# A decoder layer in one launch: next keys loaded in two halves behind the reciprocals, a later total, direct last sums, reordered fills and a double-buffered output projection

## The reference, cut to what matters

```python
# 1. self attention of the normalised x, blockwise softmax, no mask
attn = softmax(q @ k.T / sqrt(32)) @ v        # q, k, v = layernorm(x) @ w_qkv.T
x1 = x + attn @ w_out.T
# 2. causal cross attention of layernorm(x1) to 154 context rows
x2 = x1 + softmax(mask(q2 @ k2.T / sqrt(32))) @ v2 @ Wo.T + bo
# 3. shared feed forward on all rows, and the best of 8 experts on 1024 selected rows
out = x2 + ffn(layernorm(x2))
```

## Time and profile before

| | us or share |
|---|---|
| median of 3 runs (lowest, highest) | 3226.08 (3216.08, 3235.38) |
| profiled execution: its own time, its span | 3223.79, 3221.8 |
| PE busy | 2954.7, 92% |
| DVE busy | 2101.2, 65% |
| POOL busy | 1751.7, 54% |
| ACT busy | 1608.9, 50% |
| mean granted PE clock, as a share of 2.4 GHz | 0.946 |

### The profile page before, as it was taken

One profiled execution on the slowest core, in us unless ns is written; L12 is line 12 of the kernel. 1 busy time (PEld: TensorE's weight loads), 2 busy tenths in 40 slices (PEclk: granted clock), 3 DMA queues, 4 the chain that ended last, 5 costly groups with the idle time before them and its releaser, 6 DMA issues. The chain is left out here.

```text
span 3221.8 us, 42178 instructions
## 1 busy us (share of the span) xinstructions
PE 2954.7 (92%) x15214; PEld 1739.5 (54%) x15214; DVE 2101.2 (65%) x3804; ACT 1608.9 (50%) x2996; POOL 1751.7 (54%) x750
## 2 busy tenths in 40 slices
PE   8999699999999999999999999959959997999398
PEld 5878355455455454554554555338845554777333
DVE  4332777777777677777777777526638895776323
ACT  2222166666666676666666676722217673222111
POOL 0000179788889798888888888830001101432265
PEclk9999599999999999999999999979969998999589
DMA  7444744745655557457456564438665452342621
GB/s 229 173 179 157 184 103 98 161 99 111 149 112 121 129 106 157 96 107 151 97 114 143 112 143 93 96 105 247 210 169 154 139 146 93 140 169 97 217 68 36
DMA packets 186936, 435.77 MB, mean 135 GB/s; under 512 B 30557, under 2 KB 51966, under 8 KB 166716
## 3 DMA queue, kind: packets, MB, share of 16 engines
q1 hardware_dynamic: 161718, 286.39, 30.7%
q0 software_dynamic: 24448, 145.80, 21.5%
q10 hardware_dynamic: 576, 1.05, 0.1%
HBM read 180.67 MB, written 127.18 MB: 96 GB/s over the span
## 5 line engine op out<-in xcount | busy, mean ns | idle before, releaser
L791 DVE TENSOR_REDUCE part_max<-ps_s 128x1 f32<-128x512 f32 x2048 | 1270.2, 683 | 349.6 <-PE ps_s L692 349.6
L891 ACT ACTIVATE probs<-ps_st 128x512 f32<-128x512 f32 x2048 | 1059.6, 602 | 538.2 <-PE ps_st L711 529.4
L641 POOL TENSOR_TENSOR added<-added,probs 128x2048 f32<-128x2048 f32 x256 | 1181.1, 4614 | 104.6 <-ACT probs L891 82.3
L711 PE MATMUL ps_st<-q_stack,k_stack 98*128 98x512 f32 x2048 | 871.5, 429 | 8.3 <-ACT probs L891 7.0
L692 PE MATMUL ps_s<-k_stack,q_stack 96*128 96x512 f32 x2048 | 831.5, 412 | 24.2 <-POOL max_parts L631 20.7
L711 PEld LDWEIGHTS ps_st<-q_stack,k_stack 98*128 98x128 f32 x2048 | 390.2, 191 | 524.9 <-ACT probs L891 362.0
L722 PE MATMUL ps_pv<-probs,v_sb 128*32 128x512 f32 x4096 | 550.1, 609 | 0.0
L692 PEld LDWEIGHTS ps_s<-k_stack,q_stack 96*128 96x128 f32 x2048 | 399.4, 195 | 121.7 <-DVE part_max L791 36.6
L649 POOL DMA_DIRECT2D probs<-probs x128 | 110.9, 871 | 191.9 <-PE ps_pv L722 167.0
L722 PEld LDWEIGHTS ps_pv<-probs,v_sb 128*32 128x32 f32 x4096 | 80.9, 108 | 163.6 <-ACT probs L891 134.6
L641 POOL TENSOR_TENSOR added<-probs 128x2048 f32<-128x2048 f32 x32 | 146.6, 4581 | 23.9 <-ACT probs L891 23.9
(11 more groups left out here) (273 smaller groups left out, 3534.7 us busy)
## 6 DMA issues: line engine op xcount, KB each, us to landing
probs<-probs POOLq DMA_DIRECT2D x128, 1024.0 KB, 7.2
xq_stack<-q_parts SPq DMA_DIRECT2D x64, 384.0 KB, 4.8
q_parts<-k_stack SPq DMA_DIRECT2D x88, 256.0 KB, 4.0
q_stack<-q_hi SPq DMA_DIRECT2D x64, 256.0 KB, 6.8
k_stack<-k_hi SPq DMA_DIRECT2D x64, 256.0 KB, 9.7
x_in<-in_x_rows SPq DMA_DIRECT2D x8, 1024.0 KB, 7.1
q_hi<-qk_h_out SPq DMA_DIRECT2D x8, 1024.0 KB
q_lo<-qk_l_out SPq DMA_DIRECT2D x8, 1024.0 KB, 6.3
```

Source lines behind the costliest of these rows:

```text
L641: pool.tensor_tensor(added[:, w % 2], left, probs[:, k % RING], ALU.add).then_inc(added_up, 1)
L711: pe.matmul(ps_st[:, n % BANKS], k_stack[0:TOP, w // BPB, j, k * P:(k + 1) * P], q_stack[:, w % 4, j], start=True, stop=True).then_inc(ite ...
L791: dve.tensor_reduce(part_max[:, s:s + 1], ps_s[:, (w * SLOTS + s) % BANKS], AX.X, ALU.max)\
L891: act.activation(probs[:, k % RING, j], ps_st[:, n % BANKS], ACT.Exp, scale=SCALE).then_inc(item_used, 1)
```

## The change

In self attention, the next quad's keys are loaded two heads at a time in the first two units of the current quad and its values in the third, each behind the reciprocals of the unit before and ahead of its store (`load_ahead`); the queries' loads stay at the end of a unit. `INVERT_AT` goes from 9 to 7, `PRODUCT_AFTER` from 5 to 4, chain 0's total from step 8 to 9. In the last unit POOL stops adding after tile 10 and PE sums tiles 11 to 15 directly; chain 1's total comes last. At the stage's start, POOL fills `max_parts` first and the long rows of `k_stack` last, PE starts its scores without waiting for fills, and the identity is converted with a reduce in place of a copy.

In `attention_to_queries`, `a_h` and `a_l` get two buffers, PE projects blocks 0 and 1 before the first transposes, and queries are stored as high and low only (8 transfers for a block, not 12); `cross_attention` reads the high part twice. Three fills of `cross_attention` move from DVE to POOL, and PE waits for them only where it needs them. In `shared_feed_forward`, `bo` is loaded first under its own semaphore, POOL's `add_bias(0, 0)` comes before its fills, and DVE's split of the biases comes after the first norm.

```diff
-    TOTALS_AT = {8: 0, 14: 1}
-    INVERT_AT = 9
-    PRODUCT_AFTER = 5
+    TOTALS_AT = {9: 0, 14: 1}
+    LAST_ADDED = 10
+    INVERT_AT = 7
+    PRODUCT_AFTER = 4
+    LAST_ADDS = ADDED.index(LAST_ADDED)
...
+                def load_ahead(i, w, last):
+                    c, n = w // BPB, w % BPB
+                    if last and c == 1:
...
+                    elif c == 1 or i > 0:
+                        behind = (i, BPB - 1) if c else (i - 1, UPB - 1)
+                        if n < 2:
+                            load_k(2 * i + 1 + c, 1 - c, range(2 * n, 2 * n + 2))
+                        elif n == 2:
+                            sp.wait_ge(pv_done, at(*behind, KT, KT))
+                            load_v(2 * i + 1 + c, 1 - c)
+
+                def body(i, last):
+                    for w in range(UPB):
+                        if not begins(i, w):
+                            reciprocals(*unit_before(i, w))
+                        load_ahead(i, w, last)
+                        if not begins(i, w):
+                            store(*unit_before(i, w))
+                        if not last or w < BPB:
+                            sp.wait_ge(item_done, items(i, w, item(i, w, KT - 1, HEADS - 1) + 1))
+                            load_q(i * UPB + (w + 4), w % 4, w % BPB)
...
-                        for n in range(4, ADDS):
+                        for n in range(4, LAST_ADDS if ends(i, w) else ADDS):
...
-                    if k in TOTALS_AT:
+                    if ends(i, w) and k > LAST_ADDED:
+                        for j in range(HEADS):
+                            mm = pe.matmul(ps_d[j * HD:(j + 1) * HD], ones[:], probs[:, k % RING, j], start=False, stop=False)
+                    elif k in TOTALS_AT:
...
+                def last_totals(i, w):
+                    pe.wait_ge(added_up, at(i, w, ADDS, LAST_ADDS))
+                    for j in range(HEADS):
+                        pe.matmul(ps_d[j * HD:(j + 1) * HD], ones[:], added[:, w % 2, j], start=False, stop=False)
+                    pe.wait_ge(chain_summed[1], at(i, w, 32, 32))
...
-                dve.wait_ge(ident_loaded, 16)
-                dve.tensor_copy(ident_r[:], ident[:]).then_inc(ident_ready, 1)
-                dve.wait_ge(ones_set, 3)
                 for s in range(SLOTS):
                     slot_max(0, 0, s)
                     if s == HALF - 1:
+                        dve.wait_ge(ident_loaded, 16)
+                        dve.tensor_reduce(ident_r[:], ident[:].unsqueeze(2), AX.X, ALU.max).then_inc(ident_ready, 1)
+                        dve.wait_ge(ones_set, 1)
```

The same for the later stages, cut further:

```diff
-        a_h = sb("a_h", [P, DC, BLK], F32R)
+        a_h = sb("a_h", [P, 2, DC, BLK], F32R)
...
-        Q_DMAS = 3 * (P // HD)
+        Q_DMAS = 2 * (P // HD)
...
                 split(0, 0)
                 residual(0, 0)
+                split(0, 1)
                 dve.wait_ge(small_loaded, 32)
                 norm(0, 0)
-                split(0, 1)
+                residual(0, 1)
                 transposed(0, 0, range(TPB))
...
                 project(0, 0)
+                project(0, 1)
...
-                dve.memset(q_stack[ROWS:TOP + 1].bitcast(F32), 1.0).then_inc(rows_set, 1)
-                dve.memset(kt_stack[ROWS:TOP].bitcast(F32), 1.0).then_inc(rows_set, 1)
-                dve.memset(ones[:], 1.0).then_inc(rows_set, 1)
...
-                dve.wait_ge(w_loaded, 6 * 16)
-                dve.wait_ge(consts, 3)
-                dve.tensor_copy(bias_rows[0:1], bias_raw[:]).then_inc(bias_high, 1)
```

More of the change, by code:

```diff
@@ L553, in load_q, with load_k @@
                                      q_units[part][b, g, n]).then_inc(q_loaded[buf], 16)
-                def load_k(quad, buf):
+                def load_k(quad, buf, heads=range(HEADS)):
                     b, g = quad // QUADS, quad % QUADS
-                    for j in range(HEADS):
+                    for j in heads:
                         for row, part in ((0, 0), (1, 0), (2, 1)):
@@ L587, in store @@
                     sp.dma_start(out_units[b, g, w % BPB], attn_out[:, w % 2]).then_inc(out_stored[w % 2], 16)
[L589 to L595, removed]
-                            load_k(i * 2 + (c + 2), c)
-                            sp.wait_ge(pv_done, at(i, w, KT, KT))
-                            load_v(i * 2 + (c + 2), c)
-                        if last and w == BPB - 1:
+                def load_ahead(i, w, last):
+                    c, n = w // BPB, w % BPB
+                    if last and c == 1:
+                        if n == 0:
                             sp.wait_ge(next_w_copied, 32)
@@ L620, in _ @@
                 body(TURNS - 1, True)
+                store(TURNS - 1, UPB - 1)
                 for s in range(2):
@@ L673, in body @@
                                 product(*unit_before(i, w))
+                        if ends(i, w):
+                            product(*unit_before(i, w))
                 body(0)
@@ L737, in added_totals @@
                         mm = pe.matmul(ps_d[j * HD:(j + 1) * HD], ones[:], added[:, w % 2, j], start=False, stop=True)
+                    mm.then_inc(dens_done, 1)
+                def last_totals(i, w):
+                    pe.wait_ge(added_up, at(i, w, ADDS, LAST_ADDS))
+                    for j in range(HEADS):
+                        pe.matmul(ps_d[j * HD:(j + 1) * HD], ones[:], added[:, w % 2, j], start=False, stop=False)
+                    pe.wait_ge(chain_summed[1], at(i, w, 32, 32))
+                    for j in range(HEADS):
+                        mm = pe.matmul(ps_d[j * HD:(j + 1) * HD], ones[:], probs[:, CHAINS[1][-1] % RING, j],
+                                       start=False, stop=True)
                     mm.then_inc(dens_done, 1)
@@ L1069, in _ @@
                 pool.wait_ge(group_low, NBLK * DC)
-                store_part(pool, NBLK // 2 - 1, 1, 1, last_stored)
+                store_part(pool, NBLK // 2 - 1, 1, 1, range(2, 4), last_stored)
             @block.vector
@@ L1126, in body @@
                     if not last:
-                        residual(i2, u2)
+                        if not first(i, u):
+                            residual(i2, u2)
                         norm(i2, u2)
@@ L1149, in split @@
                         act.wait_ge(a_loaded[u], i * 16 + 16 * u)
-                        act.wait_ge(proj_done, count(i, u, TPB, 0))
-                    act.activation(a_h[:], first_a if first(i, u) else a_raw[:, u], ACT.Copy).then_inc(a_high, 1)
+                    if not (isinstance(i, int) and i == 0):
+                        act.wait_ge(proj_done, count(i, u, TPB, -TPB))
+                    act.activation(a_h[:, u], first_a if first(i, u) else a_raw[:, u], ACT.Copy).then_inc(a_high, 1)
                 def transposed(i, u, tiles):
@@ L1216, in body @@
                     i2, u2 = (i, 1) if u == 0 else (i + 1, 0)
-                    if not last:
+                    if not (last or first(i, u)):
                         project(i2, u2)
```

128 lines of the change are left out of this document (69 added, 59 removed).

## The result

The changed kernel takes 3191.67 us (median of 4 runs, 3189.63 to 3194.97) against 3230.73 for the kernel before (4 runs): ratio 0.988, 95% interval 0.9859 to 0.9902. It is 39 us faster; 70.6 were forecast, and 3191.67 lies above the range (3143 to 3184).

The account below looks back on a forecast made before the run. PE was taken to set the pace in self attention, losing 44.6 us at quad starts. That, 16 for the last unit and smaller terms, less collisions and other losses, summed to 70.6 us gained: 3156 us, range 3143 to 3184.

Parts of the forecast that it names:

- The keys in two halves: Self attention: smaller key loads behind the reciprocals remove PE's stalls in the first unit of each new quad; gain 44.6 us.
- The later total: Self attention: chain 0's total one step later removes PE's small waits for links; gain 2 us.
- The opening of self attention: PE waits for its first head's keys instead of POOL's fills; gain 2.5 us (0 to 4).
- The stores behind the projection with the opening of cross attention: Fewer query stores left at the output projection's end, 5 us, and cross attention's first scores waiting for loads alone, 4 us.
- what the half loads collide with: Self attention: key loads briefly overlap chain 1's links; loss 3 us, bounds nothing and 18 us.
- rival A: The collision moves into 18 ordinary units, 1.5 us each: 3179 us; chance 0.10, or 0.04 beyond the point where it turns slower.
- The last unit: End of self attention: shorter link wait, PE's direct sums and no wait for POOL's last adds; gain 16 us (6 to 21).
- Output projection: Its head: projecting block 1 ahead of block 0's transposes leaves these exposed; loss 2 us (1 to 4).
- Feed forward: Its opening: the third projected tile's wait for a residual goes; gain 1.5 us (-1 to 2.5).
- B: Rival: DVE waits at its earlier inversion and PE behind it, 1 us in each of 31 units: 3187 us; chance 0.05.
- C: Rival: quad stalls go, but the last unit gives only 6 us and openings meet the next wait: 3176 us; chance 0.09.
- D: Rival: the 44.6 us at the quad's start have another cause than these loads: about 3200 us; chance 0.04.

Follow-up runs that it names:

- e9: The kernel before with SP's schedule alone changed: keys two heads at a time and values, loaded at the head of the unit; 3187.99 us, ratio 0.987.
- e2: The changed kernel with the loads of keys, values and next weights issued ahead of the unit's reciprocals, not behind them; 3153.30 us, ratio 0.9778.
- e8: e2 with the planner's three numbers set back: chain 0's total at step 8, inversion at 9, product after add 5; 3165.16 us.
- e1: The changed kernel with all loads ahead issued behind the unit's reciprocals and its store, not between the two; 3156.15 us, ratio 0.9785.
- e6: e2 with the last unit's sums as before: POOL adds all tiles and PE makes one total behind them; 3167.86 us.
- e10: e2 with the output projection's old opening order, and POOL's bias adds for block 1 ahead of its reciprocal roots; 3148.32 us, ratio 0.9745.
- e11: The changed kernel with all four heads of a quad's keys (3 MB) loaded at once, at the same place behind the reciprocals; 3215.86 us.

## Why the prediction was wrong

**What held.** The keys in two halves: 44.6 us forecast, 45.3 measured (e9, with the loads at e2's place). The inversion is at 22.4 us of each of the units 1 to 30 with no idle time before it. The later total in units 1 to 30: 2 forecast; the three planner numbers together give 3.2 (e9 to e2) to 4.8 (e8), and the total alone was not tried. The opening of self attention, 2.5 and 3.1, with the first score at 340.7 us as forecast. The stores behind the projection with the opening of cross attention, 9 and 9.8: from the last group to the next stage's first load it is 12.1 us and was 18.3, 6.2 gained for 5.3, and from there to the first score 11.8 and was 15.5, 3.6 gained for 4.

**The step that failed** is "what the half loads collide with", 3 us, which came out at 38 (e2, where units 1 to 30 take 1567.6 us for 1605.7; 39 by e1): some 31 in the key units and 7 in unit 28. That is 35 of the 42 us by which the traces miss the forecast gain. It was rival A, at 2.7 us in 12 units for my 1.5 in 18; the units with values lost nothing. The mechanism was named, with the right link, the right reader and its slack of 1 us; its size was wrong, by three inputs. First the keys' start: 29 us took the start of the reciprocals' issues to move by the full 6.5 us (to 27.0; it is 28.2 to 29.2) and their price from a row at 33.5 us, where the four take 1.7 us and not 3.4 to 4.8. So the keys start at 32.1 to 33.2 us and end their flight near 43 us and not at 38 to 39.5. The overlap was over 5 us and not 1 to 2, and by ACT's wait the link of unit 12 landed at 47.6 us and not at 44.4: 3.2 us late, of which the slack covers 1. Second, the upper bound of 18 us priced PE's stand alone, at 1 us; it is 1.6 us on average, and the work at the lower clock behind it adds about 1 us on average (near nothing in six units, 1.8 to 2.0 us in the others). Third, unit 28 had no term: that `load_ahead` also moves 3 MB of the next stage from a unit's end to the same place stood in the diff.

**The last unit**, 16 forecast and 10.8 measured. The sum gave 6 us for PE's wait at chain 0's total and its lower clock. The step that failed here is that this wait would fall to some 0.5 us. It left that reader and stood with another: ACT wants the ring place that the same link reads, one step later, and stood 3.37 us (with the old sums, 3.42, e6). With the old sums the unit still takes 49.2 us (e6) where it took 49.8, so the 6 us came out at 0.6; the direct sums add 3.4 to it, where 2.1 were taken. The end behind it gave 13.6 us (27.4 to 13.8) for 12.2. By e10 some 2.4 us of the unit hang on whether the clock falls behind that wait.

**Output projection**, -2 and -3.4, inside its 1 to 4.

**Cross attention** lost 3.2 us behind an opening that came 3.6 us earlier. The fourth unit's queries stand in SP's queue behind the first two units' rows. Their load lands at 2380.1 us, and PE goes on at once; it stood for 3.11 us there, and for 2.16 us before:

```profile
2380.19 0.47 PE L1469 MATMUL xps_s<-xks_stack,xq_stack 96*128 96x154 f32 x1 [3.11 <-issue]
```

The 31.4 us to the first unit's end became 34.6. In the other kernels with the new opening it was 33.4 to 37.1 (37.1 in e10, which loses its gain there). The whole stage takes 299.8 to 306.5 us with the new opening and 297.6 and 298.1 (the kernel before and e9) with the old one. So the new opening costs it, and I had given it no term. The longer wait is only 1 us of the 3.2; where the rest goes was not tried.

**Feed forward**, 1.5 and -0.7. In the nine kernels with the changed opening the stage takes 294.8 to 298.4 us, so the term is -0.1 to -3.7, a loss and not the gain of 1.5; -1 lies inside that. The larger part of the cost lay with the norms and the cast, of which the term said nothing: they take 4.01 and 1.74 us beside POOL's adds, 1.92 and 0.67 without them (e10), and the subtraction 2.17 and 1.22. The Trainium skill, "SBUF — State Buffer", section "Who interferes with whom", has a VectorE instruction with two inputs in SBUF contend with GpSimd's reads, and names cast and `tensor_scalar` as able to take the ports that the two engines share; the traces agree with both by these numbers.

**Rivals.** B (the inversion waits) is out: DVE has no wait for the denominators in units 1 to 30 of the changed kernel. C is out: the last unit and its end gave 10.8 us where C has 6, and two of the openings gave 3.1 and 9.8 (with the stores) where C has nothing. What C says, that the next wait is met, did hold in the feed forward and in the last unit. D is out by e9. The 1.8 us behind the feed forward are no effect: what follows its last output transpose took 227 to 234 us in the kernels of this study, whose code there is the same.

## What to carry to other kernels

A load that is moved must be priced where it lands, by the transfers in flight there, and with its issue times taken from a row of the same part of the period: the row at 33.5 us was no price for the place at 28. In a periodic schedule write down the flights of all transfers that someone soon waits for, over one period (here 10.7 to 17.5, 21 to 28, 26 to 33, 37.5 to 44.4 us, and the small ones from 16 to 32), and put the bulk into the longest gap; here that is around the unit's border, and it was worth 38 us more than the change's place. When a wait is removed by a later reader, look for the next reader of the same transfer, and when work goes from ahead of a hand-over to behind it, look at who runs beside it now.

## What the runs showed of the hardware

- What SP needs to issue the same transfers changes with the place. The four loads of the reciprocals take 3.4 to 4.8 us at 28 us after a unit's start, while a link that POOL issued is in flight, and 1.7 us at 33.5, after it has landed; six key loads take 2.8 to 4.5 us at 32 us and 2.8 to 3.5 us at 44.6 (e1). A link in flight alone does not make it so: e11 issues three key loads in 0.42 us each just behind the issue of a link, and e2 needs 3.7 to 4.2 us for six with none in flight. The cause was not tried.
- A bulk load on another queue halves the speed of a transfer: a link takes 6.9 us alone and 13.4 beside SP's loads. The Trainium skill, "DMA: Bandwidth & Descriptors", section "Queues, rings and completion order", has each engine take turns between the queues that have work; the trace agrees.
- A stand of PE costs its own length and, where PE goes on at half clock, some 2 to 6 us more. In the changed kernel 1.82 us became 3.8 in unit 12 and 4.49 became 7.3 in unit 28; in e11 6.94 became 9.5; in the kernel before 5.65 us, in two stands, became 11.3 in unit 12. But 1.72 us in unit 17 cost 2.0 at full clock, and 1.58 in unit 5 cost 3.4: among stands of 1.4 to 1.8 us the length does not tell which it is.
